# Low parts of W ahead of tile 0's gate, and tile 0's LoRA and tile 1's narrow product inside tile 1's wide product

## Chip, core and metric

The kernel runs on one core of a Trainium2 chip. The metric is the device time of one execution in microseconds (us); the lower the better. Times of the trace are us from the start of the span.

## What is computed

The input x has 1024 rows of 1024 numbers, handled as 8 tiles of 128 rows. First a quantised product with the context is added to x, then an FFN with a top-2 LoRA mixture on the layer-normalised result:

```
x1 = x + fake_quant(layernorm(x)) @ fake_quant(ctx)      # 2 batches, 1024 x 1024 ctx each
y = layernorm(x1)
logits = y @ W_router.T;  combine = renormalised top 2 of softmax(logits)   # 8 experts
h = (y @ A_stack.T) * combine                            # 8 experts x rank 16 = 128 columns
out = x1 + y @ W_base.T + b_base + (h @ B_stack) * 2
```

## The kernel before

There is no scheduler: each engine runs a list of calls written out by hand, in order, and waits on semaphores. An instruction that waits holds up all that stands behind it in its engine's list.

Stage 1 (`product`, L795) makes x1 tile by tile; VectorE adds the product to x (`sum_x1`, L541), and a correction row is added by `add_corr`: for tiles 0 to 2 on VectorE (L550), for tiles 3 to 7 on POOL (L250).

Stage 2 works in float16 pairs: each float32 operand is split into a high part (ScalarE) and a low part (VectorE), and TensorE multiplies high by high, high by low, low by high. For each tile t:

- The layer norm of y: `statistics_y` on VectorE (L464 to L466), `scale_y` on POOL (nine small operations, L261 to L289), `make_y` on ScalarE (L383).
- The transposed y: tiles 0 and 1 are transposed by TensorE (`transpose_y`, L804) and split by `split_first_yt` or `split_yt`. From tile 2 on, ScalarE rounds y to its high part (`round_y`, L402), VectorE makes the low part (`rest_y`, L637), and two DMA transposes of SyncE's queue bring `yt_hi` and `yt_lo` (L205, L207).
- `narrow(t)` (L816 to L818, 24 small matmuls) gives the 128 LoRA columns and 8 logits in one PSUM bank.
- `gate_tile(t)` on VectorE (L642 to L655, with one exp on ScalarE, `gate_weight`, L406) turns the logits into `hc`, which TensorE transposes (`transpose_hc`, L810). `split_hct` splits the result (ScalarE L410, VectorE L662).
- `wide(t, k)` for k = 0 to 7 (L835, 6 matmuls each) is the base product with slice k of W. For tile 0 it waits for `w_lo` of slice k, which VectorE makes from `w_hi` (`split_w`, L606 and L370).
- `lora(t)` (L825, 6 matmuls) adds the LoRA part; then VectorE's `sum_out` (L677) adds the product to x1, `add_bias` (L671) has added the bias, and the tile is stored.

`keep_busy` (L845) issues matmuls whose result is not used, between stage 1 and stage 2. From tile 2 on `narrow(t)` waits for both DMA transposes of its tile. In ScalarE's list before, the step of tile t is:

```
for t in range(1, T):
    gate_weight(t)
    if t + 1 < T:
        make_y(t + 1)
        round_y(t + 1)
    split_hct(t)
```

Of the kernel before, what the change touches and what calls it, by code (L numbers as in the profile page):

```python
# [5 lines left out]
P = 128  # L6
# [3 lines left out]
F32 = mybir.dt.float32  # L10
# [19 lines left out]
def xattn_ffn(nc, x, ctx_kv, quant, w_t, bias, ar_t, b_t, out):  # L30
# [20 lines left out]
    with ExitStack() as stack:  # L51
# [83 lines left out]
        YT_BANKS = slice(6, 8)  # L135
        OUT_BANK = [0, 4]
        AR_BANK = 2
        HCT = slice(256, 256 + P)
        LAST_PIECES = ((0, H), (H, H + H // 2), (H + H // 2, D))
        PEAKS = 2 + K  # L140
        FIRST = 2
        FIRST_ADDS = 3

        quant_in = sem("quant_in")
        x0_half = sem("x0_half")
# [96 lines left out]
        @block.gpsimd  # L242
        def _(pool):
            def fill(tile):
                return nc.gpsimd.memset(tile.rearrange("p t d -> p (t d)").bitcast(U32), OFFSET_PAIR)

            def add_corr(t):
                pool.wait_ge(x1_summed, t + 1)
                pool.wait_ge(corr_ready, t // TB + 1)
                nc.gpsimd.tensor_tensor(xs[:, t, :], xs[:, t, :], corr[:, t // TB, :], ALU.add).then_inc(x1_ready, 1)  # L250

            steps = [0]

# [37 lines left out]

            nc.gpsimd.memset(ident[:, :], 0.0).then_inc(ident_ready, 1)
            pool.wait_ge(ident_ready, 1)
            nc.gpsimd.affine_select(out=ident[:, :], in_=ident[:, :], compare_op=ALU.not_equal, fill=1.0,
                                    base=0, pattern=[[-1, P]], channel_multiplier=1).then_inc(ident_ready, 1)
            then(nc.gpsimd.memset(minus_half[:, :], -0.5))
            for first, last in ((0, 4), (4, 8)):
                fill(a2[:, first:last, :]).then_inc(a2_filled, 1)
            nc.gpsimd.iota(expert_i[:, :], pattern=[[1, EX]], base=0, channel_multiplier=0).then_inc(iota_ready, 1)
            fill(a1[:, 4:8, :]).then_inc(a1_rest_filled, 1)  # L300
            fill(a2[:, 12:16, :]).then_inc(a2_filled, 1)
            pool.wait_ge(consts_ready, 1)
            pool.wait_ge(a1_filled, 2)
            pool.wait_ge(a1_rest_filled, 1)
            scale_x(1, 2)
            for t in range(2, 6):
                scale_x(t, t + 1)
                quantise_x(t)
            scale_x(6, 8)
            quantise_x(6)  # L310
            quantise_x(7)
            scale_y(0, 2)
            pool.wait_ge(b_lo_ready, 1)
            add_corr(3)
            scale_y(2, 3)
            add_corr(4)
            scale_y(3, 4)
            for t in range(5, T):
                add_corr(t)
                scale_y(t - 1, t)  # L320
            scale_y(T - 1, T)

        @block.scalar
        def _(act):
# [82 lines left out]

            def split_hct(t):
                act.wait_ge(hc_transposed, t + 1)
                nc.scalar.activation(hct_hi[:, :], ps[:, AR_BANK, HCT], ACT.Copy).then_inc(hct_hi_ready, 1)  # L410

            act.dma_start(prm[:, :], quant.partition_broadcast(P)).then_inc(quant_in, 16)
            act.wait_ge(ones_ready, 1)
# [19 lines left out]
            split_w(1)  # L433
            split_w(2)
            make_y(1)
            split_b()
            for k in range(3, K):
                split_w(k)
            gate_weight(0)
            split_yt(1)  # L440
            split_hct(0)
            sum_row(0)
            sum_row(1)
            for t in range(1, T):
                gate_weight(t)
                if t + 1 < T:
                    make_y(t + 1)
                    round_y(t + 1)
                split_hct(t)
                if t + 1 < T:  # L450
                    sum_row(t + 1)

        @block.vector
        def _(dve):
# [204 lines left out]

            def split_hct(t):  # L660
                dve.wait_ge(hct_hi_ready, t + 1)
                nc.vector.tensor_tensor(hct_lo[:, :], ps[:, AR_BANK, HCT], hct_hi[:, :].bitcast(F32),  # L662
                                        ALU.subtract).then_inc(hct_lo_ready, 1)

            def add_bias(t):
# [58 lines left out]
            sum_x1(4)  # L724
            take_a1t(6)
            scale_ar()
            add_corr(2)
            sum_x1(5)
            peaks_w()
            take_a1t(7)  # L730
            scale_w()
            split_ar()
            sum_x1(6)
            split_w(0)
            split_first_yt()
            split_w(1)
            split_w(2)
            split_w(3)
            sum_x1(7)
            dve.wait_ge(iota_ready, 1)  # L740
            nc.vector.tensor_copy(expert[:, :], expert_i[:, :]).then_inc(expert_ready, 1)
            split_w(4)
            split_w(5)
            dve.wait_ge(expert_ready, 1)
            gate_tile(0)
            split_w(6)
            split_w(7)
            split_hct(0)
            split_b()
            split_yt(1)  # L750
            statistics_y(2)
            add_bias(0)
            for t in range(1, T):
                gate_tile(t)
                sum_out(t - 1)
                split_hct(t)
                add_bias(t)
                if t + 1 < T:
                    rest_y(t + 1)
                if t + 2 < T:  # L760
                    statistics_y(t + 2)
# [11 lines left out]
        def _(pe):  # L773
# [33 lines left out]

            def transpose_hc(t):
                pe.wait_ge(hc_ready, t + 1)
                nc.tensor.transpose(ps[:, AR_BANK, HCT], hc[:, :], ident[:, :]).then_inc(hc_transposed, 1)  # L810

            def narrow(t):
                dst = ps[:, AR_BANK, 0:AR]
# [80 lines left out]
                    if t + 1 < T and k == 4:  # L894
                        transpose_a1(t + 1)

            keep_busy(6, 5)
            pe.wait_ge(x1_summed, T - 1)
            pe.wait_ge(first_half_lo, 1)
            for k in range(K):  # L900
# [2 lines left out]
                pe.wait_ge(w_lo_ready, k + 1)  # L903
                wide(0, k, False)
                if k == 3:
                    pe.wait_ge(x1_summed, T)
                    pe.wait_ge(yt_lo_ready, 1)
                    pe.wait_ge(ar_lo_ready, 2)
                    narrow(0)
                if k == 3:  # L910
                    transpose_y(1)
                if k == 5:
                    transpose_hc(0)
            pe.wait_ge(b_lo_ready, 1)
            lora(0, stop=True)

            for t in range(1, T - 1):
                if t == 1:
                    pe.wait_ge(yt_lo_ready, 2)
                else:  # L920
                    pe.wait_ge(y_hi_turned, 16 * (t - 1))
                    pe.wait_ge(y_lo_turned, 16 * (t - 1))
                narrow(t)
                if t >= 2:
                    pe.wait_ge(out_summed, t - 1)
                for k in range(K):
                    wide(t, k, k == K - 1)
                    if k == 2:
# [44 lines left out]
```

## Time and profile before

| | us |
|---|---|
| median of 3 runs | 171.85 (171.85 to 171.87) |
| the profiled execution's own time | 171.81 |
| its span, first to last instruction | 170.0 |
| TensorE busy | 158.2 (93%) |
| VectorE busy | 118.9 (70%) |
| ScalarE busy | 74.1 (44%) |
| POOL busy | 59.9 (35%) |
| mean granted TensorE clock, as a share of 2.4 GHz | 0.996 |

The profiled execution took 1.8 us beyond its span. Busy shares are means over the whole span; the stages have different limits, so a stage has to be read from its own stretch.

### The profile page before, as it was taken

How to read it: one execution, taken by the hardware profiler on the slowest of the kernel's cores; microseconds unless marked ns; L12 is line 12 of the kernel's file. 1: busy time of each engine (PE TensorE's matmuls, PEld its weight loads, DVE VectorE, ACT ScalarE, POOL GpSimd, SP SyncE). 2: the span in 40 equal slices, each digit the busy share in tenths (PEclk: the TensorE clock that was granted, in tenths of full speed). 3: DMA queues.
4: the chain of work that ended last, by engine and by line, in shares of the span. 5: the costliest groups of instructions: out<-in, count | busy, mean ns of one | idle time of the engine just before them, and what ended most of it. 6: DMA issues, size and time to landing. Idle time of an engine off the chain costs nothing.

```text
span 170.0 us, 2585 instructions
## 1 busy us (share of the span) xinstructions
PE 158.2 (93%) x922; PEld 83.6 (49%) x922; DVE 118.9 (70%) x276; ACT 74.1 (44%) x100; POOL 59.9 (35%) x140
## 2 busy tenths in 40 slices
PE   6977898899989799799999999999999999999992
PEld 3543344345535356364554564564555556456541
DVE  7993939999998999996919908908907826804802
ACT  3096509799996994506217007105305305300000
POOL 8905476887840000187082081082050050000000
PEclk9999999999999999999999999999999999999998
DMA  4999999999930000000352250350360360360311
GB/s 111 387 416 413 406 409 407 406 411 413 407 151 2 0 0 4 0 0 0 75 177 41 46 160 10 72 169 0 62 185 4 62 185 0 62 185 6 123 62 62
DMA packets 19452, 25.89 MB, mean 152 GB/s; under 512 B 13552, under 2 KB 13808, under 8 KB 19440
## 3 DMA queue, kind: packets, MB, share of 16 engines
q1 hardware_dynamic: 19296, 25.73, 43.4%
q8 instruction: 7, 0.11, 0.3%
q14 instruction: 5, 0.04, 0.1%
q10 hardware_dynamic: 144, 0.00, 0.0%
HBM read 18.38 MB, written 4.19 MB: 133 GB/s over the span
## 4 chain that ended last, share of the span: by engine, by line
PE 62%; DVE 19%; issue 6%; POOL 5%; ACT 4%; DMA 2%; DVEq 0%; ACTq 0%; POOLq 0%
PE ps L835 37%; PE ps L795 10%; PE ps L825 5%; DVE w_lo L606 2%; PE ps L786 2%; DVE xs L541 2%; ACT w_hi L370 2%; DMA yt_lo<-a_t 2%; PE ps L816 2%; PE ps L817 2%; PE ps L818 2%; POOL root L262 2%; PE ps L780 1%; DVE bnx L472 1%; DVE bnx L470 1%
## 5 line engine op out<-in xcount | busy, mean ns | idle before, releaser
L835 PE MATMUL ps<-w_hi,yt_hi 128*128 128x512 f16 x128 | 39.5, 380 | 1.7 <-DVE w_lo L606 1.2
L835 PE MATMUL ps<-w_lo,yt_hi 128*128 128x512 f16 x128 | 39.4, 379 | 0.0
L835 PE MATMUL ps<-w_hi,yt_lo 128*128 128x512 f16 x128 | 39.4, 379 | 0.0
L795 PE MATMUL ps<-a,a_t 128*128 128x512 f16 x128 | 31.2, 379 | 2.3 <-DVE a_t L534 1.5
L406 ACT ACTIVATE gate<-gate,ar_undo 128x1 f32<-128x1 f32 x8 | 2.4, 295 | 55.9 <-DVE gate L643 55.9
L331 ACT ACTIVATE a<-stage,prm,inv_s 128x1024 uint8<-128x1024 f32 x16 | 19.4, 1241 | 9.4 <-DMA stage<-in_ctx_kv 9.3
L642 DVE MAX8 top<-ps 128x8 f32<-128x8 f32 x8 | 1.4, 173 | 27.5 <-PE ps L818 27.5
L835 PEld LDWEIGHTS ps<-w_hi,yt_lo 128*128 128x128 f16 x128 | 12.5, 98 | 15.1
L795 PEld LDWEIGHTS ps<-a,a_t 128*128 128x128 f16 x128 | 11.9, 98 | 16.2 <-DVE a_t L534 3.0
L835 PEld LDWEIGHTS ps<-w_lo,yt_hi 128*128 128x128 f16 x128 | 12.5, 98 | 14.7
L250 POOL TENSOR_TENSOR xs<-xs,corr 128x1024 f32<-128x1024 f32 x5 | 11.8, 2363 | 22.2 <-DVE b_lo L612 22.2
L835 PEld LDWEIGHTS ps<-w_hi,yt_hi 128*128 128x128 f16 x128 | 11.6, 98 | 14.9 <-issue 2.8
L261 POOL TENSOR_SCALAR root<-mvy 128x1 f32<-128x1 f32 (+1 forms) x7 | 1.5, 218 | 38.8 <-DVE mvy L466 38.7
L816 PE MATMUL ps<-ar_hi,yt_hi 128*128 128x136 f16 x64 | 11.7, 223 | 0.2 <-DMA yt_lo<-a_t 0.2
L817 PE MATMUL ps<-ar_lo,yt_hi 128*128 128x136 f16 x64 | 11.7, 223 | 0.0
L818 PE MATMUL ps<-ar_hi,yt_lo 128*128 128x136 f16 x64 | 11.7, 223 | 0.0
L383 ACT ACTIVATE y<-xs,y_bias,y_scale 128x1024 f32<-128x1024 f32 x8 | 9.8, 1228 | 1.8 <-POOL y_bias L289 1.8
L671 DVE SCALAR_TENSOR_TENSOR xs<-xs,row_term,bias_sb 128x1024 f32<-128x1024 f32 x8 | 10.3, 1285 | 0.3
L786 PE MATMUL ps<-a,ones 128*128 128x512 f16 x32 | 9.5, 379 | 0.9 <-ACT a L331 0.9
L606 DVE SCALAR_TENSOR_TENSOR w_lo<-stage,scale,w_hi 128x1024 f16<-128x1024 f32 x8 | 10.0, 1279 | 0.2 <-ACT w_hi L370 0.2
L541 DVE SCALAR_TENSOR_TENSOR xs<-ps,con,xs 128x1024 f32<-128x1024 f32 x8 | 10.1, 1268 | 0.0
L262 POOL TENSOR_TENSOR root<-root,minus_half 128x1 f32<-128x1 f32 (+1 forms) x13 | 9.7, 744 | 1.1
(135 smaller groups left out, 262.4 us busy)
## 6 DMA issues: line engine op xcount, KB each, us to landing
stage<-in_ctx_kv SPq DMA_DIRECT2D x16, 512.0 KB, 13.2
stage<-in_w_t SPq DMA_DIRECT2D x8, 512.0 KB, 10.7
xs<-in_x SPq DMA_DIRECT2D x7, 512.0 KB, 13.2
out_dram<-xs SPq DMA_DIRECT2D x7, 512.0 KB, 3.0
ar_raw<-in_ar_t SPq DMA_DIRECT2D x1, 544.0 KB, 16.3
xs<-in_x SPq DMA_DIRECT2D x2, 256.0 KB, 3.8
b_raw<-in_b_t SPq DMA_DIRECT2D x1, 512.0 KB, 11.3
bias_sb<-in_bias SPq DMA_DIRECT2D x1, 512.0 KB, 12.1
```

The lines of the kernel that those rows point to most:

```text
L250: nc.gpsimd.tensor_tensor(xs[:, t, :], xs[:, t, :], corr[:, t // TB, :], ALU.add).then_inc(x1_ready, 1)
L262: then(nc.gpsimd.tensor_tensor(guess, whole, minus_half[:, w], ALU.pow))
L331: nc.scalar.activation(low_bytes(a2[:, n, :]), stage[:, n % RING, :], ACT.Identity, bias=prm[:, 3:4], scale=inv_s[:, 2:3]).then_inc(ctx_re ...
L541: nc.vector.scalar_tensor_tensor(out=xs[:, t, :].rearrange("p (h n) -> p h n", h=NH), in0=ps[:, s1_bank(t):s1_bank(t) + 2, :], scalar=s12, ...
L606: nc.vector.scalar_tensor_tensor(out=w_lo[:, k, :], in0=stage[:, k, :], scalar=scale[:, 2:3], in1=w_hi[:, k, :], op0=ALU.mult, op1=ALU.sub ...
L671: nc.vector.scalar_tensor_tensor(out=xs[:, t, :], in0=xs[:, t, :], scalar=row_term[:, t:t + 1], in1=bias_sb[:, :], op0=ALU.add, op1=ALU.ad ...
L786: last = nc.tensor.matmul(ps[:, COLSUM_BANK + h, :], ones16[:, 0:P], a2[:, b * K + k, h * H:(h + 1) * H], start=k == 0, stop=k == K - 1)
L795: last = nc.tensor.matmul(ps[:, s1_bank(t) + h, :], a1_t[:, t % 4, k, :], a2[:, n, h * H:(h + 1) * H], start=k == 0, stop=k == K - 1)
L816: nc.tensor.matmul(dst, yt_hi[:, p, k, :], ar_hi[:, k, :], start=k == 0, stop=False)
L817: nc.tensor.matmul(dst, yt_hi[:, p, k, :], ar_lo[:, k, :], start=False, stop=False)
L818: last = nc.tensor.matmul(dst, yt_lo[:, p, k, :], ar_hi[:, k, :], start=False, stop=k == K - 1)
L835: ins = nc.tensor.matmul(ps[:, OUT_BANK[p] + h, :], part, rhs[:, k, h * H:(h + 1) * H], start=k == 0 and part is hi and rhs is w_hi, stop= ...
```

## The change

VectorE no longer adds the correction of tile 2; POOL does, once `w_diag_ready` is set, and on POOL `scale_y` now stands ahead of `add_corr` of the next tile. VectorE makes the low parts of the LoRA and router weights (`split_ar`) after `w_lo` of slice 3, makes all `w_lo` and tile 1's `yt_lo` ahead of tile 0's gate, and reads `a1_t` of tile 7 ahead of `peaks_w`. TensorE runs `narrow(0)` after `wide(0, 5)`, and all of `transpose_hc(0)`, `narrow(1)`, `lora(0)` and `transpose_hc(1)` inside tile 1's wide product; `lora(1)` ends it. The transposed `hc` gets a PSUM bank of its own. For tile 1 alone, `split_hct(1)` stands ahead of `make_y(2)` and `round_y(2)` on ScalarE, and ahead of `sum_out(0)` on VectorE. `keep_busy` issues 2 matmuls in the place of 6.

```diff
-        FIRST_ADDS = 3
+        FIRST_ADDS = 2
...
             scale_y(0, 2)
+            pool.wait_ge(w_diag_ready, 1)
+            add_corr(2)
             pool.wait_ge(b_lo_ready, 1)
-            add_corr(3)
-            scale_y(2, 3)
-            add_corr(4)
-            scale_y(3, 4)
-            for t in range(5, T):
+            for t in range(3, T):
+                scale_y(t - 1, t)
                 add_corr(t)
-                scale_y(t - 1, t)
             scale_y(T - 1, T)
...
             make_y(1)
-            split_b()
             for k in range(3, K):
                 split_w(k)
+            split_yt(1)
+            split_b()
             gate_weight(0)
-            split_yt(1)
             split_hct(0)
             sum_row(0)
             sum_row(1)
             for t in range(1, T):
                 gate_weight(t)
+                if t == 1:
+                    split_hct(t)
                 if t + 1 < T:
                     make_y(t + 1)
                     round_y(t + 1)
-                split_hct(t)
+                if t > 1:
+                    split_hct(t)
...
             scale_ar()
-            add_corr(2)
             sum_x1(5)
+            take_a1t(7)
             peaks_w()
-            take_a1t(7)
             scale_w()
-            split_ar()
             sum_x1(6)
             split_w(0)
             split_first_yt()
             split_w(1)
             split_w(2)
             split_w(3)
+            split_ar()
+            split_w(4)
             sum_x1(7)
...
-            split_w(4)
-            split_w(5)
+            for k in range(5, K):
+                split_w(k)
+            split_yt(1)
             dve.wait_ge(expert_ready, 1)
             gate_tile(0)
-            split_w(6)
-            split_w(7)
             split_hct(0)
             split_b()
-            split_yt(1)
             statistics_y(2)
             add_bias(0)
             for t in range(1, T):
                 gate_tile(t)
-                sum_out(t - 1)
-                split_hct(t)
+                if t == 1:
+                    split_hct(t)
+                    sum_out(t - 1)
+                else:
+                    sum_out(t - 1)
+                    split_hct(t)
...
-            keep_busy(6, 5)
+            keep_busy(2, 5)
...
                 wide(0, k, False)
                 if k == 3:
+                    transpose_y(1)
+                if k == 5:
                     pe.wait_ge(x1_summed, T)
-                    pe.wait_ge(yt_lo_ready, 1)
                     pe.wait_ge(ar_lo_ready, 2)
                     narrow(0)
+
+            pe.wait_ge(yt_lo_ready, 2)
+            for k in range(K):
+                wide(1, k, False)
+                if k == 1:
+                    transpose_hc(0)
+                if k == 2:
+                    narrow(1)
                 if k == 3:
-                    transpose_y(1)
-                if k == 5:
-                    transpose_hc(0)
-            pe.wait_ge(b_lo_ready, 1)
-            lora(0, stop=True)
-
-            for t in range(1, T - 1):
...
+                    pe.wait_ge(b_lo_ready, 1)
+                    lora(0, stop=True)
+                if k == 6:
+                    transpose_hc(1)
+            lora(1, stop=True)
```

On ScalarE, the end of the list for tiles 0 and 1 before: the exp of a gate is L406, the high part of the transposed `hc` L410, `y` of the next tile L383 and its rounding (named `a_t` by the memory it shares) L402.

```order
L406 ACTIVATE gate<-gate,ar_undo 128x1
L394 ACTIVATE yt_hi<-ps 128x1024
L410 ACTIVATE hct_hi<-ps 128x128
L345 ACTIVATE junk,rowsum<-a1 128x1024 x2
L406 ACTIVATE gate<-gate,ar_undo 128x1
L383 ACTIVATE y<-xs,y_bias,y_scale 128x1024
L402 ACTIVATE a1_t<-y 128x1024
L410 ACTIVATE hct_hi<-ps 128x128
L345 ACTIVATE junk,rowsum<-a1 128x1024
```

The same place in the changed kernel, whose lines stand one lower (L405, L409, L382, L401):

```order
L393 ACTIVATE yt_hi<-ps 128x1024
L374 ACTIVATE b_hi<-b_raw 128x1024
L405 ACTIVATE gate<-gate,ar_undo 128x1
L409 ACTIVATE hct_hi<-ps 128x128
L344 ACTIVATE junk,rowsum<-a1 128x1024 x2
L405 ACTIVATE gate<-gate,ar_undo 128x1
L409 ACTIVATE hct_hi<-ps 128x128
L382 ACTIVATE y<-xs,y_bias,y_scale 128x1024
L401 ACTIVATE a1_t<-y 128x1024
L344 ACTIVATE junk,rowsum<-a1 128x1024
```

The high part of tile 1's transposed `hc` has moved ahead of tile 2's `y` and its rounding.

On TensorE, tile 1's wide product (L835) around the transpose of its `hc` (L810), before; the list goes on with the rest of `lora(1)` (L825) and two more slices of W:

```order
L835 MATMUL ps<-w_hi,yt_lo 128x512 x2
L810 MATMUL ps<-ident,hc 128x128
L835 MATMUL ps<-w_hi,yt_hi 128x512 x2
L835 MATMUL ps<-w_lo,yt_hi 128x512 x2
L835 MATMUL ps<-w_hi,yt_lo 128x512 x2
L835 MATMUL ps<-w_hi,yt_hi 128x512 x2
L835 MATMUL ps<-w_lo,yt_hi 128x512 x2
L835 MATMUL ps<-w_hi,yt_lo 128x512 x2
L835 MATMUL ps<-w_hi,yt_hi 128x512 x2
L835 MATMUL ps<-w_lo,yt_hi 128x512 x2
L835 MATMUL ps<-w_hi,yt_lo 128x512 x2
L825 MATMUL ps<-b_hi,hct_hi 128x512 x2
```

The end of tile 1 in the changed kernel, where these are L839, L814 and L829, up to tile 2's narrow product:

```order
L839 MATMUL ps<-w_lo,yt_hi 128x512 x2
L839 MATMUL ps<-w_hi,yt_lo 128x512 x2
L839 MATMUL ps<-w_hi,yt_hi 128x512 x2
L839 MATMUL ps<-w_lo,yt_hi 128x512 x2
L839 MATMUL ps<-w_hi,yt_lo 128x512 x2
L814 MATMUL ps<-ident,hc 128x128
L839 MATMUL ps<-w_hi,yt_hi 128x512 x2
L839 MATMUL ps<-w_lo,yt_hi 128x512 x2
L839 MATMUL ps<-w_hi,yt_lo 128x512 x2
L829 MATMUL ps<-b_hi,hct_hi 128x512 x2
L829 MATMUL ps<-b_lo,hct_hi 128x512 x2
L829 MATMUL ps<-b_hi,hct_lo 128x512 x2
```

The transpose of tile 1's `hc` has moved from behind slice 2 to behind slice 6; one slice and `lora(1)` follow it, and then comes `narrow(2)`.

On VectorE, from the weight scale to tile 0's gate, before (`ar_lo` is `split_ar`, L541 `sum_x1`, L619 tile 0's `yt_lo`, L642 the gate's first operation):

```order
L586 SCALAR_TENSOR_TENSOR ar_lo<-ar_raw,scale,ar_hi 128x8x128
L586 SCALAR_TENSOR_TENSOR ar_lo<-ar_raw,scale,ar_hi 128x8x8
L541 SCALAR_TENSOR_TENSOR xs<-ps,con,xs 128x1024
L606 SCALAR_TENSOR_TENSOR w_lo<-stage,scale,w_hi 128x1024
L619 TENSOR_TENSOR yt_lo<-ps,yt_hi 128x512 x2
L606 SCALAR_TENSOR_TENSOR w_lo<-stage,scale,w_hi 128x1024 x3
L541 SCALAR_TENSOR_TENSOR xs<-ps,con,xs 128x1024
L741 CAST expert<-expert_i 128x8
L606 SCALAR_TENSOR_TENSOR w_lo<-stage,scale,w_hi 128x1024 x2
L642 MAX top<-ps 128x8
```

The same in the changed kernel (L588, L543, L608, L621, L630 for tile 1's `yt_lo`, L644 for the gate):

```order
L543 SCALAR_TENSOR_TENSOR xs<-ps,con,xs 128x1024
L608 SCALAR_TENSOR_TENSOR w_lo<-stage,scale,w_hi 128x1024
L621 TENSOR_TENSOR yt_lo<-ps,yt_hi 128x512 x2
L608 SCALAR_TENSOR_TENSOR w_lo<-stage,scale,w_hi 128x1024 x3
L588 SCALAR_TENSOR_TENSOR ar_lo<-ar_raw,scale,ar_hi 128x8x128
L588 SCALAR_TENSOR_TENSOR ar_lo<-ar_raw,scale,ar_hi 128x8x8
L608 SCALAR_TENSOR_TENSOR w_lo<-stage,scale,w_hi 128x1024
L543 SCALAR_TENSOR_TENSOR xs<-ps,con,xs 128x1024
L743 CAST expert<-expert_i 128x8
L608 SCALAR_TENSOR_TENSOR w_lo<-stage,scale,w_hi 128x1024 x3
L630 TENSOR_TENSOR yt_lo<-ps,yt_hi 128x1024
L644 MAX top<-ps 128x8
```

`split_ar` is now behind four `w_lo`, and the gate begins only after the eighth and after tile 1's `yt_lo`.

## Rows read from the trace of the kernel before

**Rows 1.** Busy time by stretch: us, busy (instructions) of each engine, then clock, DMA
```profile
55.60:87.00 31.40, 29.49 (x178) 15.87 (x177) 27.03 (x52) 16.23 (x22) 9.39 (x17) 1.00 0.12 31
86.70:100.00 13.30, 13.28 (x79) 7.25 (x80) 8.76 (x20) 3.80 (x6) 5.05 (x14) 1.00 0.35 97
```

**Rows 2.** The chain that ended last: start us, us, what
```profile
53.15 0.89 PE ps L804 x8
...
65.22 0.18 DVE top L642
...
67.49 0.29 DVE hc L655
...
72.64 0.60 DVE bny L464
...
77.77 0.22 POOL y_bias L289
...
80.31 0.27 ACT hct_hi L410
...
80.81 0.28 DVE row_term L667
...
82.31 1.23 DVE a_t L637
83.56 3.03 DMA yt_lo<-a_t
...
86.72 0.22 PE ps L816
...
88.30 3.88 PE ps L835 x18
...
96.26 1.39 PE ps L825 x6
```

**Rows 3.** Timeline of TensorE: start us, us, operation, idle before and its releaser
```profile
51.20 0.23 PE L878 MATMUL ps<-diag,ones_b 128*128 128x128 bf16 x1 [0.85 <-DVE a_t L534]
...
57.30 0.59 PE L835 MATMUL ps<-w_hi,yt_hi 128*128 128x512 f16 x2 [0.57 <-DVE yt_lo L619]
...
88.14 0.59 PE L835 MATMUL ps<-w_hi,yt_hi 128*128 128x512 f16 x2
```

**Rows 4.** Timeline of VectorE, same columns
```profile
47.70 1.23 DVE L550 TENSOR_TENSOR xs<-xs,corr 128x1024 f32<-128x1024 f32 x1
...
51.46 0.29 DVE L597 TENSOR_REDUCE power<-ps 128x1 f32<-128x128 f32 x1 [0.32 <-PE ps L878]
...
52.73 1.48 DVE L586 SCALAR_TENSOR_TENSOR ar_lo<-ar_raw,scale,ar_hi 128x1024 f16<-128x1024 f32 x2
...
56.52 1.28 DVE L619 TENSOR_TENSOR yt_lo<-ps,yt_hi 128x512 f16<-128x512 f32 x2
57.71 2.48 DVE L606 SCALAR_TENSOR_TENSOR w_lo<-stage,scale,w_hi 128x1024 f16<-128x1024 f32 x2
```

**Rows 5.** Timeline of ScalarE, same columns
```profile
52.79 1.15 ACT L370 ACTIVATE w_hi<-stage,scale 128x1024 f16<-128x1024 f32 x1 [1.25 <-DVE scale L601]
...
58.24 1.05 ACT L375 ACTIVATE b_hi<-b_raw 128x1024 fp32r<-128x1024 f32 x1
```

**Rows 6.** Timeline of POOL, the add of tile 5's correction
```profile
87.86 2.36 POOL L250 TENSOR_TENSOR xs<-xs,corr 128x1024 f32<-128x1024 f32 x1
```

**Rows 7.** Timeline of VectorE during that add
```profile
88.55 0.21 DVE L643 TENSOR_SCALAR gate<-top 128x1 f32<-128x1 f32 x1
...
88.95 1.30 DVE L646 CAST top_f<-top_i 128x8 f32<-128x8 uint32 x1
```

**Rows 8.** Busy time by stretch at the end of the span
```profile
165.75:167.00 1.25, 0.96 (x5) 0.45 (x3) 0.26 (x1) 0.00 (x0) 0.00 (x0) 1.00 0.00 0
168.50:169.00 0.50, 0.00 (x0) 0.00 (x0) 0.00 (x0) 0.00 (x0) 0.00 (x0) 0.68 0.80 270
```

**Rows 9.** The source line of the first 32 matmuls: duration ns min/median/max, first and last start
```profile
L842 PE MATMUL ps<-ones x32: 326/326/527, 1.4 to 8.1; 128*128 128x384 f16 x32
```

More of the change, by code:

```diff
@@ L137, in xattn_ffn @@
         AR_BANK = 2
-        HCT = slice(256, 256 + P)
+        HCT_BANK = 3
+        HCT = slice(0, P)
         LAST_PIECES = ((0, H), (H, H + H // 2), (H + H // 2, D))
@@ L409, in split_hct @@
                 act.wait_ge(hc_transposed, t + 1)
-                nc.scalar.activation(hct_hi[:, :], ps[:, AR_BANK, HCT], ACT.Copy).then_inc(hct_hi_ready, 1)
+                nc.scalar.activation(hct_hi[:, :], ps[:, HCT_BANK, HCT], ACT.Copy).then_inc(hct_hi_ready, 1)
             act.dma_start(prm[:, :], quant.partition_broadcast(P)).then_inc(quant_in, 16)
@@ L661, in split_hct @@
                 dve.wait_ge(hct_hi_ready, t + 1)
-                nc.vector.tensor_tensor(hct_lo[:, :], ps[:, AR_BANK, HCT], hct_hi[:, :].bitcast(F32),
+                nc.vector.tensor_tensor(hct_lo[:, :], ps[:, HCT_BANK, HCT], hct_hi[:, :].bitcast(F32),
                                         ALU.subtract).then_inc(hct_lo_ready, 1)
@@ L809, in transpose_hc @@
                 pe.wait_ge(hc_ready, t + 1)
-                nc.tensor.transpose(ps[:, AR_BANK, HCT], hc[:, :], ident[:, :]).then_inc(hc_transposed, 1)
+                nc.tensor.transpose(ps[:, HCT_BANK, HCT], hc[:, :], ident[:, :]).then_inc(hc_transposed, 1)
             def narrow(t):
@@ L905, in _ @@
                 if k == 3:
+                    transpose_y(1)
+                if k == 5:
                     pe.wait_ge(x1_summed, T)
-                    pe.wait_ge(yt_lo_ready, 1)
                     pe.wait_ge(ar_lo_ready, 2)
                     narrow(0)
-                if k == 3:
-                    transpose_y(1)
-                if k == 5:
-                    transpose_hc(0)
-            pe.wait_ge(b_lo_ready, 1)
-            lora(0, stop=True)
-            for t in range(1, T - 1):
[L918 to L922, printed above, removed]
+            pe.wait_ge(yt_lo_ready, 2)
[5 more added lines that the diff above has]
+                    narrow(1)
+                if k == 3:
+                    pe.wait_ge(b_lo_ready, 1)
[3 more added lines that the diff above has]
+            lora(1, stop=True)
+            for t in range(2, T - 1):
+                pe.wait_ge(y_hi_turned, 16 * (t - 1))
+                pe.wait_ge(y_lo_turned, 16 * (t - 1))
                 narrow(t)
-                if t >= 2:
-                    pe.wait_ge(out_summed, t - 1)
+                pe.wait_ge(out_summed, t - 1)
                 for k in range(K):
```

## The prediction

> **What bounds the kernel now.** I read the busy time by stretch first. From 86.7 us on TensorE is busy for 13.28 us of 13.30 us [rows 1]: one tile of stage 2, and so on to the end; nothing but fewer or slower matmuls changes that part. Ahead of it, from 55.6 to 87.0 us, where tiles 0 and 1 run, it is busy for 29.49 of 31.40 us. So about 2 us can be had there, and some in the wait just before (below). Then the chain that ended last, which says what sets the start of the full part. It is not TensorE. Through 72.64, 77.77, 80.31, 82.31 and 83.56 us it runs over VectorE's statistics of tile 2, POOL's scale, ScalarE, VectorE's low part of y and the DMA transpose of `yt_lo`, and releases `narrow(2)` at 86.72 us [rows 2]. TensorE had only just finished tile 1: two limits meet here. Any gain in tiles 0 and 1 arrives at 86.72 us only if tile 2's y comes sooner too. The chain also shows that before 86.72 us VectorE had waited for ScalarE's part of tile 1's transposed `hc` (80.31 us) ahead of that low part: the two chains, gate and y, are tied.
>
> **The front of stage 2.** The W peak matmul stood at 51.20 us after 0.85 us of idle, for VectorE's `a1_t` of tile 7 [rows 3]. Without `add_corr(2)` (47.70 us, 1.15 us in the queue beside 1.23 long) [rows 4] and with `take_a1t(7)` ahead of `peaks_w`, VectorE is done in time, and TensorE's own products set the start: 51.20 - 0.85 = 50.3 us, 0.9 us sooner. Everything to the weight scale moves with it. `split_ar` leaves the path: it stood at 52.73 us, 1.48 us long, 1.4 us in the queue [rows 4]. Tile 0's `yt_lo` then starts at 56.52 - 0.9 - 1.4 = 54.2 us, and `wide(0, 0)`, which began 0.78 us behind it (57.30 us [rows 3]), at 55.0 us. With 2 `keep_busy` instead of 6 TensorE is free by then: it was free at 57.30 - 0.57 = 56.7 us, less 0.9, less four of 384 columns at 2.4 GHz, 0.16 us each, gives 55.2 us at most. Gain so far 2.2 us.
>
> **Tiles 0 and 1 on TensorE.** Costs of one: `wide` 3.88 / 3 = 1.29 us, `lora` 1.39, eight transposes of y 0.9 [rows 2]; `narrow` 88.14 - 86.72 = 1.42 us [rows 2, 3]; a transpose of `hc` 0.1 us by the same eight. Waits for `w_lo`, each 1.28 us long and 1.2 us in the queue (two took 2.48 us [rows 4]): slice 1 starts at 54.2 + 1.2 and is ready at 56.7, TensorE wants it at 56.3 (wait 0.4). Slice 3 needs its `w_hi`, which takes the place of `split_b`: 58.24 - 0.9 = 57.3 us, 1.15 us long [rows 5], so `w_lo` is ready at 59.8 against 59.4 (0.4). Slice 4 comes behind `split_ar`, ready at 62.4 against 62.0 (0.4). Slice 5 comes behind `sum_x1(7)`, ready at 64.9 against 63.7 (1.2). Slices 6 and 7 are made while `narrow(0)` runs. Sum of waits 2.4 us; moving the gate behind all `w_lo` does not remove them, since `split_ar` and `sum_x1(7)` still stand between.
>
> Up to the transpose of tile 1's `hc` there are 15 `wide` (19.4), two `narrow` (2.8), one `lora` (1.4), y (0.9) and `hc` (0.1): 24.6 us. It starts at 55.0 + 24.6 + 2.4 = 82.1 us. One `wide` and `lora(1)` remain: TensorE is done with tiles 0 and 1 at 82.1 + 0.1 + 1.3 + 1.4 = 84.9 us.
>
> Is `hc` of tile 1 there by then? Tile 0's transpose, behind two slices of tile 1, is at about 72.8 us, so VectorE's `split_hct(0)` starts at about 73.6; `b_lo` (1.2), statistics (1.5) and `add_bias` (1.5) bring the gate to 77.8, and it takes 67.49 + 0.29 - 65.22 = 2.6 us [rows 2]: 80.4 us. Yes. Tile 2's scale: statistics from 74.8 us, and y_bias came 5.35 us behind their start (72.64 to 77.99 [rows 2]), so 80.2 us, 2 us later than before; hidden, because of the next step.
>
> **The step that decides: `split_hct(1)` ahead of `make_y(2)`.** ScalarE keeps its order, so y of tile 2 cannot be made before the transpose at 82.1 us. Add: 0.3 us to ScalarE's reading it (0.26 us for the peak matmul, 51.20 to 51.46 [rows 3, 4]); from there VectorE's `row_term` came 0.5 us later (80.31 to 80.81), and now `sum_out(0)` stands between, another 1.2 us by an operation of that size; 1.5 us to the low part of y, 1.25 us to its DMA, 3.16 us to `narrow(2)` (80.81, 82.31, 83.56, 86.72) [rows 2]. Sum 0.3 + 0.5 + 1.2 + 1.5 + 1.25 + 3.16 = 7.9 us, so `narrow(2)` starts at 90.0 us. The high part is no later: y and its rounding took 80.31 - 77.99 = 2.3 us, ready at 82.1 + 0.5 + 2.4 = 85.0, and VectorE reaches `rest_y` at 85.6. The two DMAs of SyncE's queue are then some 1.9 us apart, and I take the second's 3.16 us as unchanged; if it waited for the whole of the first, which takes about as long, it would be 1.2 us later. SyncE itself is free: its wait for `lora(0)` ends at about 78 us, and tile 0's store stands behind both. Under this chain TensorE has 2.8 us of work and stands idle for 5.1 us.
>
> So `narrow(2)` is 90.0 - 86.72 = 3.3 us later, with all of tiles 2 to 7 behind it at the old pace: each later tile's y chain starts from its own gate, in the old order. POOL's adds have slack there (2.36 us [rows 6] in a tile of 13.3 us). 171.81 (this execution's own time; 0.04 under the median) + 3.3 = 175.1 us at full clock. Lower bound of this term: no wait for `w_lo` at all gives 79.7 + 7.9 = 87.6, still +0.9, 172.7 us.
>
> **The clock.** After its last matmul, at 165.75 + 0.96 = 166.7 us, TensorE's granted clock was down to half inside the stretch 168.5 to 169.0 us (mean 0.68, so at about 168.7) [rows 8]: after some 2 us without work it went from 2.4 to 1.2 GHz. An idle of 5 us in mid-kernel should see the same, once at least. Price from the start of the kernel: 32 matmuls of 384 columns started from 1.4 to 8.1 us [rows 9], 31 steps in 6.7 us where 0.16 us each makes 5.0: 1.7 us lost before the clock was up (the longest took 527 ns, the median 326). I take 1.6 us; bounds 0, since the rise could come early after the gap, and 3.3, an estimate for a low stretch of twice the length. Sum 171.81 + 3.3 + 1.6 = 176.7 us.
>
> The Trainium skill, "TensorE: Matmul & The Clock Gate", HAM oscillation, says that idle gaps between bursts of matmuls throw the array back to the low clock and that the next burst starts cold. By that rule, with which the tail of this trace agrees, the sum is 176.7; without it, 175.1.
>
> **Rivals.**
> *The clock stays up* (0.17): all as above, 175.1 us. For it: the old kernel's waits, 0.85 and 0.57 us [rows 3], left the clock at 1.00; against it, they are short.
> *POOL's add holds VectorE up* (0.06): `add_corr(2)` now runs from about 50.3 to 52.7 us, beside the scale's small operations on VectorE. In the old trace a cast of 128x8 took 1.30 us and ended as such an add ended, 90.2 us; but a TENSOR_SCALAR of 128x1, the form the scale is made of, took its usual 0.21 us during it [rows 6, 7]. If they do wait, the scale, whose first such operation is due at 51.46 + 0.29 - 0.9 = 50.9 us [rows 4], is 52.7 - 50.9 = 1.8 us later and everything with it: 176.9, or 178.5 with the clock. The Trainium skill, "SBUF — State Buffer", Who interferes with whom, lets `tensor_scalar` among others take the port that VectorE shares with POOL, and speaks against this add there; the 0.21 us row speaks for it.
> *The y chain is less late* (0.04): waits for `w_lo` largely gone, 172.7 to 174.5 us.
> *Faster* (0.04): tile 2's y is there when TensorE ends tile 1 at 84.9 us, so the full part starts 1.8 us sooner: 170.0 us. It decides from a transpose of tile 1's `hc` earlier than 86.72 - 7.9 = 78.8 us, and TensorE's work alone puts it at 79.6. Only a far shorter tail, say the DMA at half its 3.16 us, together with no waits, would do it; nothing in the rows shows either.
>
> **How the numbers follow.** The likeliest case, late y and a fallen clock, has 0.69, 175.6 to 178.2 by the bounds of its clock term; I give 176.7. The range takes in the rival at full clock: 175.0 to 178.2, leaving out the less late, the faster, and part of the POOL case. A change of 0.2%, 0.35 us, is about what a measurement here can tell. Slower by more 0.95, within it 0.01, faster 0.04.
>
> **What would show it.** `wide(0, 0)` near 55.0 us; waits for `w_lo` ahead of slices 1, 3, 4, 5; ScalarE idle until the second transposed `hc` near 82 us with POOL's bias ready at 80; `yt_lo`'s DMA issued near 86.9; TensorE idle from 85 to 90 us, released by that DMA; granted clock under 1.00 around 87 to 93. If `narrow(2)` starts before 87 us I am wrong in the step that decides; if the clock stays 1.00, in the last term.

## The result, and the profile after

The changed kernel takes 177.65 us in the median of 4 runs (177.18 to 178.0), the kernel before 171.85 us. The ratio is 1.0336, with a 95% interval of 1.0311 to 1.0361: slower by 5.8 us. The profiled execution, the longest of the four, took 178.0 us over a span of 176.2 us, 6.2 us more span than before.

The page of the changed kernel, its span and the slices of TensorE and of its clock:

```profile
span 176.2 us, 2577 instructions
...
PE   6997889899999979999359999999999999999992
...
PEclk9999999999999999999966999999999999999999
```

There are two dents. In slices 20 and 21 (84 to 93 us) TensorE is busy for three and five tenths, and in slices 21 and 22 its clock is at six tenths. The waits of TensorE name the first:

```profile
PE ps L820 <- DMA yt_lo<-a_t: 5.0, 1, 5.0
PE ps L839 <- DVE w_lo L608: 1.8, 4, 0.9
```

One wait of 5.0 us, for tile 2's `yt_lo`, and four for `w_lo`. The timeline of TensorE, with the waits in brackets:

```profile
50.33 0.22 PE L882 MATMUL ps<-diag,ones_b 128*128 128x128 bf16 x1
...
55.09 0.59 PE L839 MATMUL ps<-w_hi,yt_hi 128*128 128x512 f16 x2
...
56.83 0.60 PE L839 MATMUL ps<-w_hi,yt_hi 128*128 128x512 f16 x2 [0.29 <-DVE w_lo L608]
...
64.93 0.60 PE L839 MATMUL ps<-w_hi,yt_hi 128*128 128x512 f16 x2 [0.92 <-DVE w_lo L608]
...
82.23 0.27 PE L814 MATMUL ps<-ident,hc 128*128 128x128 f32 x1
...
90.16 0.27 PE L820 MATMUL ps<-ar_hi,yt_hi 128*128 128x136 f16 x1 [4.98 <-DMA yt_lo<-a_t]
```

The peak matmul comes 0.87 us sooner than in [rows 3], stage 2 starts at 55.09 in the place of 57.30 us, and tile 1 is done at 85.18 us (84.56 + 0.62 for its last two matmuls). In the kernel before, it was done at 86.53 us, the start of `narrow(2)` less the idle ahead of it:

```profile
86.72 0.22 PE L816 MATMUL ps<-ar_hi,yt_hi 128*128 128x136 f16 x1 [0.19 <-DMA yt_lo<-a_t]
```

So TensorE is done with tiles 0 and 1 1.35 us sooner. But `narrow(2)` starts at 90.16 in the place of 86.72 us. VectorE ahead of it in the changed kernel, each row with its start and duration as above:

```profile
82.84 0.29 DVE L664 TENSOR_TENSOR hct_lo<-ps,hct_hi 128x128 fp32r<-128x128 f32 x1 [2.58 <-ACT hct_hi L409]
83.05 1.27 DVE L679 SCALAR_TENSOR_TENSOR xs<-ps,con,xs 128x1024 f32<-128x1024 f32 x1
84.24 0.26 DVE L669 TENSOR_SCALAR row_term<-rowsum,con 128x1 f32<-128x1 f32 x1
84.54 1.28 DVE L673 SCALAR_TENSOR_TENSOR xs<-xs,row_term,bias_sb 128x1024 f32<-128x1024 f32 x1
85.74 1.22 DVE L639 TENSOR_TENSOR a_t<-y,a_t 128x1024 f16<-128x1024 f32 x1
```

VectorE sat idle for 2.58 us ahead of `hct_lo` of tile 1, and between that and the low part of tile 2's y (the last row) stand three more operations. ScalarE over the same time:

```profile
82.53 0.28 ACT L409 ACTIVATE hct_hi<-ps 128x128 fp32r<-128x128 f32 x1 [4.10 <-PE ps L814]
82.71 1.23 ACT L382 ACTIVATE y<-xs,y_bias,y_scale 128x1024 f32<-128x1024 f32 x1
84.03 1.06 ACT L401 ACTIVATE a_t<-y 128x1024 f16<-128x1024 f32 x1
```

ScalarE, too, waited for the transpose, and had y rounded at 85.09 us, 0.65 us before VectorE reached the low part. Both lists hold y behind the transpose of `hc`; VectorE's holds it a little longer. Then the clock, by stretches of 1 us (the third number from the end is the granted clock, ahead of the DMA's share and its GB/s):

```profile
88.00:89.00 1.00, 0.00 (x0) 0.00 (x0) 0.36 (x2) 0.00 (x0) 0.43 (x2) 1.00 0.87 169
89.00:90.00 1.00, 0.00 (x0) 0.00 (x0) 0.00 (x0) 0.00 (x0) 0.76 (x4) 0.53 1.13 339
...
94.00:95.00 1.00, 1.00 (x4) 0.32 (x3) 0.89 (x5) 0.96 (x1) 0.00 (x0) 0.50 0.00 0
95.00:96.00 1.00, 1.00 (x4) 0.40 (x3) 0.93 (x4) 0.93 (x1) 0.00 (x0) 0.55 0.03 8
96.00:97.00 1.00, 1.00 (x7) 0.45 (x5) 0.83 (x1) 0.13 (x1) 0.00 (x0) 1.00 0.00 0
```

The clock went from 2.4 to 1.2 GHz at about 89.1 us (a mean of 0.53 over the stretch from 89 to 90 us), 3.9 us after TensorE's last work, and came back at 95.9 us. TensorE worked at 1.2 GHz from 90.16 to 95.9 us, 5.7 us, and did what takes half as long, 2.9 us, at 2.4 GHz. So 3.44 us of late start and 2.9 us of half speed are 6.3 us, against 6.2 us in the span.

### The profile page after: what moved, and what is told of

Read it like the earlier page. It is cut to its first block, busy times and chain, and to the rows that moved or that the text cites. A ratio compares the mean times of both kernels' runs of the same rounds, so it can differ in the third digit from the quotient of the medians.

```text
span 176.2 us, 2577 instructions
## 1 busy us (share of the span) xinstructions
PE 161.3 (92%) x918; PEld 85.4 (48%) x918; DVE 116.8 (66%) x275; ACT 74.1 (42%) x100; POOL 61.1 (35%) x141
## 4 chain that ended last, share of the span: by engine, by line
PE 71%; DVE 16%; POOL 3%; issue 3%; ACT 3%; DMA 2%; DVEq 0%; ACTq 0%; POOLq 0%
PE ps L839 44%; PE ps L799 10%; PE ps L829 6%; PE ps L820 2%; PE ps L821 2%; PE ps L822 2%; PE ps L790 2%; DVE xs L543 2%; DVE w_lo L608 2%; ACT w_hi L369 2%; DMA yt_lo<-a_t 2%; PE ps L784 1%; DVE bnx L474 1%; DVE bnx L472 1%; DVE a L694 1%
## 5 line engine op out<-in xcount | busy, mean ns | idle before, releaser
L839 PE MATMUL ps<-w_hi,yt_hi 128*128 128x512 f16 x128 | 40.2, 386 | 1.8 <-DVE w_lo L608 1.8
L839 PE MATMUL ps<-w_hi,yt_lo 128*128 128x512 f16 x128 | 39.8, 383 | 0.0
L839 PE MATMUL ps<-w_lo,yt_hi 128*128 128x512 f16 x128 | 39.8, 383 | 0.0
L405 ACT ACTIVATE gate<-gate,ar_undo 128x1 f32<-128x1 f32 x8 | 2.4, 295 | 56.5 <-DVE gate L645 56.5
L644 DVE MAX8 top<-ps 128x8 f32<-128x8 f32 x8 | 1.4, 172 | 29.2 <-PE ps L822 29.2
L839 PEld LDWEIGHTS ps<-w_hi,yt_lo 128*128 128x128 f16 x128 | 12.6, 99 | 15.4 <-issue 0.6
L839 PEld LDWEIGHTS ps<-w_lo,yt_hi 128*128 128x128 f16 x128 | 12.7, 99 | 15.2 <-issue 0.8
L839 PEld LDWEIGHTS ps<-w_hi,yt_hi 128*128 128x128 f16 x128 | 11.6, 99 | 15.5 <-issue 3.2
L820 PE MATMUL ps<-ar_hi,yt_hi 128*128 128x136 f16 x64 | 12.8, 234 | 5.0 <-DMA yt_lo<-a_t 5.0
L251 POOL TENSOR_TENSOR xs<-xs,corr 128x1024 f32<-128x1024 f32 x6 | 14.1, 2350 | 1.8 <-DVE diag L556 1.8
L821 PE MATMUL ps<-ar_lo,yt_hi 128*128 128x136 f16 x64 | 12.8, 235 | 0.0
L822 PE MATMUL ps<-ar_hi,yt_lo 128*128 128x136 f16 x64 | 12.8, 234 | 0.0
L608 DVE SCALAR_TENSOR_TENSOR w_lo<-stage,scale,w_hi 128x1024 f16<-128x1024 f32 x8 | 10.0, 1280 | 0.6 <-ACT w_hi L369 0.6
L543 DVE SCALAR_TENSOR_TENSOR xs<-ps,con,xs 128x1024 f32<-128x1024 f32 x8 | 10.1, 1269 | 0.1
L382 ACT ACTIVATE y<-xs,y_bias,y_scale 128x1024 f32<-128x1024 f32 x8 | 9.8, 1227 | 0.0
L820 PEld LDWEIGHTS ps<-ar_hi,yt_hi 128*128 128x128 f16 x64 | 6.6, 103 | 6.2 <-issue 5.4
```

The costliest lines, as they stand in the source:

```text
L382: nc.scalar.activation(y[:, :], xs[:, t, :], ACT.Identity, bias=y_bias[:, t:t + 1], scale=y_scale[:, t:t + 1]).then_inc(y_ready, 1)
L543: nc.vector.scalar_tensor_tensor(out=xs[:, t, :].rearrange("p (h n) -> p h n", h=NH), in0=ps[:, s1_bank(t):s1_bank(t) + 2, :], scalar=s12, ...
L608: nc.vector.scalar_tensor_tensor(out=w_lo[:, k, :], in0=stage[:, k, :], scalar=scale[:, 2:3], in1=w_hi[:, k, :], op0=ALU.mult, op1=ALU.sub ...
L820: nc.tensor.matmul(dst, yt_hi[:, p, k, :], ar_hi[:, k, :], start=k == 0, stop=False)
L821: nc.tensor.matmul(dst, yt_hi[:, p, k, :], ar_lo[:, k, :], start=False, stop=False)
L822: last = nc.tensor.matmul(dst, yt_lo[:, p, k, :], ar_hi[:, k, :], start=False, stop=k == K - 1)
```

## The experiments

All ratios are against the kernel before, run on the same chip in the same session.

**1. ScalarE's order for tile 1 undone alone.**

```diff
                 gate_weight(t)
-                if t == 1:
-                    split_hct(t)
                 if t + 1 < T:
                     make_y(t + 1)
                     round_y(t + 1)
-                if t > 1:
-                    split_hct(t)
+                split_hct(t)
```

> The changed kernel with ScalarE's order for tile 1 undone alone: y of tile 2 and its rounding again stand ahead of the high part of tile 1's transposed hc. Theory A (VectorE's list is the tie: hct_lo(1), sum_out(0), bias, low part of y): y is made from 80.2 us instead of 82.7, but hct_lo(1) still waits for the transpose at 82.2 us and for ScalarE behind the rounding (about 82.6 us), so the low part of y stays at about 85.8 us, narrow(2) at 90.2 us, and the time at 177.6 us. Theory B, my prediction's wording (ScalarE's order is what decides): y is 2.4 us sooner and narrow(2) comes at about 87.8 us, time 174.4 to 175.5 us.

Measured: 177.28 us (176.65 to 178.08), ratio 1.032 (1.0283 to 1.0358). ScalarE's timeline, then VectorE's:

```profile
80.31 1.24 ACT L382 ACTIVATE y<-xs,y_bias,y_scale 128x1024 f32<-128x1024 f32 x1 [1.83 <-POOL y_bias L290]
81.64 1.06 ACT L401 ACTIVATE a_t<-y 128x1024 f16<-128x1024 f32 x1
82.60 0.26 ACT L409 ACTIVATE hct_hi<-ps 128x128 fp32r<-128x128 f32 x1
```

```profile
82.89 0.29 DVE L661 TENSOR_TENSOR hct_lo<-ps,hct_hi 128x128 fp32r<-128x128 f32 x1 [2.58 <-ACT hct_hi L409]
...
85.80 1.22 DVE L636 TENSOR_TENSOR a_t<-y,a_t 128x1024 f16<-128x1024 f32 x1
```

y is made 2.4 us sooner, and the low part is where it was. Theory B falls: ScalarE's order, to which my prediction gave the decision, costs nothing as long as the low part of y stands behind `hct_lo(1)` in VectorE's list. The converse was not run: with VectorE's order alone changed, the low part would wait for ScalarE's rounding, done at 85.09 us in the changed kernel, so by these rows only some 0.7 us could come of it. To free y, both lists have to be changed (experiment 4).

**2. The gap filled with matmuls.**

```diff
             lora(1, stop=True)
+            keep_busy(30, 6)
```

> The changed kernel with 30 matmuls of 384 columns, whose result is not used, between the end of tile 1 and narrow(2): 30 x 0.163 = 4.9 us of work in 5.1 us of idle. Theory A (the loss is 3.4 us of late y plus 2.9 us of half clock after the idle): the clock stays at 1.00, narrow(2) still at 90.2 us, time 171.85 + 3.4 = 175.3 us, about 2.4 us under the changed kernel. Theory B (the clock is not what costs; tile 2 is slower for another reason, such as its operands or the DMA): time stays at 177.6 us.

Measured: 175.8 us (175.66 to 176.07), ratio 1.0235 (1.0218 to 1.0252), 1.9 us under the changed kernel. The start of `narrow(2)` there:

```profile
90.76 0.22 PE L820 MATMUL ps<-ar_hi,yt_hi 128*128 128x136 f16 x1 [0.65 <-DMA yt_lo<-a_t]
```

The granted clock is 1.00 in each stretch from 84 to 97 us, and the part behind is at its old pace: 174.0 - 90.76 = 83.2 us, before 170.0 - 86.72 = 83.3, in the changed kernel 176.2 - 90.16 = 86.0. The cost of the clock is shown: 2.8 us, against 2.9 worked out above. The time fell by 1.9 us only, and misses theory A's 175.3 us by 0.5, since `narrow(2)` is 0.6 us later than in the changed kernel: SyncE's issue of the first DMA transpose took 2.24 us instead of 1.31, and held the second. Why it did, no run settles; another issue took 2.00 us at 148.7 us of the same trace, far from the filling matmuls.

**3. Both orders undone.** Experiment 1, and on VectorE:

```diff
-                if t == 1:
-                    split_hct(t)
-                    sum_out(t - 1)
-                else:
-                    sum_out(t - 1)
-                    split_hct(t)
+                sum_out(t - 1)
+                split_hct(t)
```

> The changed kernel with both orders for tile 1 undone: on ScalarE y(2) and rounding first, on VectorE sum_out(0) ahead of hct_lo(1). Theory A (the late transpose of tile 1's hc is the root, at 82.2 us, and hct_lo(1) holds the low part of y whatever stands ahead of it): sum_out(0) moves into VectorE's idle, worth 1.2 us; low part at 84.5, narrow(2) at 89.0 us, TensorE idle 3.9 us, clock falls still in most runs: 176.2 to 176.6 us. Theory B (the two orders for tile 1 are the cause): undoing them brings the time back to 172 us or less.

Measured: 175.66 us (175.54 to 176.67), ratio 1.0243 (1.0211 to 1.0275). `sum_out(0)` now runs in VectorE's idle, the rest is as late as the transposed `hc`:

```profile
80.18 1.27 DVE L676 SCALAR_TENSOR_TENSOR xs<-ps,con,xs 128x1024 f32<-128x1024 f32 x1
82.85 0.29 DVE L661 TENSOR_TENSOR hct_lo<-ps,hct_hi 128x128 fp32r<-128x128 f32 x1 [1.39 <-ACT hct_hi L409]
```

`narrow(2)` came at 88.96 us as expected, TensorE idle for 3.8 us. The time is 0.5 us under what I expected, since the low clock cost less: it lasted from about 89.7 to 93.0 us. The two orders of the change are worth 1.2 us of `narrow(2)`. The rest is the later transpose, as long as the low part of y stands behind it; experiments 4 and 5 take these two apart.

**4. The low part of y ahead of the gate's chain.** ScalarE as in experiment 1, and on VectorE for tile 1 `rest_y(2)`, `split_hct(1)`, `sum_out(0)`, `add_bias(1)`:

```diff
                 if t == 1:
+                    rest_y(t + 1)
                     split_hct(t)
                     sum_out(t - 1)
...
-                if t + 1 < T:
+                if 1 < t < T - 1:
                     rest_y(t + 1)
```

> The changed kernel with y(2) and rounding first on ScalarE, and on VectorE the low part of y(2) ahead of hct_lo(1), sum_out(0) and the bias; the transpose of hc stays where it is. Theory A (tying the y chain to the gate chain costs the time): the low part runs at 82.7 to 83.9 us, right behind the rounding, its DMA is issued at 83.9, narrow(2) at 87.1 us, idle 1.8 us, clock stays up: 171.85 + 0.4 = 172.2 us (173.5 if the clock still falls). Theory B (the y chain is late by itself, from the statistics on): not below 175 us.

Measured: 172.39 us (172.34 to 172.67), ratio 1.0035 (1.0021 to 1.0049). With ScalarE's order undone and one operation of VectorE moved ahead of four others, 5.3 us of the 5.8 are gone, and the transpose stands where it stood (82.24 us):

```profile
82.78 1.23 DVE L636 TENSOR_TENSOR a_t<-y,a_t 128x1024 f16<-128x1024 f32 x1 [2.51 <-ACT a_t L401]
...
84.25 0.74 PE L827 MATMUL ps<-b_hi,hct_hi 128*128 128x512 f32 x2 [0.45 <-DVE hct_lo L661]
87.38 0.22 PE L818 MATMUL ps<-ar_hi,yt_hi 128*128 128x136 f16 x1 [1.48 <-DMA yt_lo<-a_t]
```

The low part is made at 82.78 in the place of 85.74 us. `lora(1)` waits 0.45 us for the low part of `hc` that now comes second, the idle ahead of `narrow(2)` is 1.48 us, and the clock stays at 1.00.

**5. The transpose of tile 1's hc one slice sooner.**

```diff
-                if k == 6:
+                if k == 5:
                     transpose_hc(1)
```

> The changed kernel with the transpose of tile 1's hc one slice of W sooner, behind slice 5 instead of 6; nothing else. Theory A (the y chain starts at that transpose): it runs at 80.9 instead of 82.2 us, and all behind it 1.3 us sooner: narrow(2) at 88.9 us, idle 3.8 us; 176.3 us if the clock falls as before, 174.0 if it stays up. Theory B (another wait of the chain, POOL's scale ready at 80.2 us, takes over at once): under 0.5 us of gain.

Four executions took 174.02, 175.49, 175.62 and 176.71 us; the ratio, 1.017 (1.012 to 1.0219), is that of the first three. In the profiled one `narrow(2)` starts at 88.91 us after 3.70 us of idle, 1.25 us sooner, as theory A says. The spread is the clock's: the mean granted clocks of the four are 1.0, 0.99, 0.99 and 0.98, and 174.0 is the forecast for a clock that stays up. With an idle of this length the clock's cost differs from execution to execution of one kernel. In the profiled one it fell at about 89.8 us, 0.8 us after TensorE had begun to work again, and was back at about 93.1 us.

**6. y of tile 2 sooner still.** Experiment 4, `transpose_hc(1)` behind slice 4, and `b_lo` and tile 2's statistics in VectorE's idle:

```diff
             gate_tile(0)
-            split_hct(0)
             split_b()
             statistics_y(2)
+            split_hct(0)
             add_bias(0)
```

> The orders of the run with the low part of y(2) first, and besides: b_lo and tile 2's statistics ahead of hct_lo(0) on VectorE, into its 2.6 us of idle there, and the transpose of tile 1's hc behind slice 4. Theory A: statistics end at 73.5 us, POOL's bias at 77.4, rounding at 79.8, low part at 81.0, its DMA lands at 84.2 us, before TensorE ends tile 1 at 85.0 us: no idle there, the full part starts at 85.0 us instead of 86.7, time 170.1 us, faster than both kernels. Theory B (a gain in front of tile 2 is lost again in tile 3, whose statistics now come later against its narrow product): a wait of 0.5 us or more ahead of narrow(3), time 170.7 us or more.

Measured: 172.24 us (172.04 to 172.72), ratio 1.0025 (1.0015 to 1.0035). Neither theory named the cause. The wait for `yt_lo` is gone, but TensorE waits twice for `hc`; beside it, VectorE's gate of tile 1 and POOL:

```profile
80.69 0.33 PE L812 MATMUL ps<-ident,hc 128*128 128x128 f32 x1 [0.89 <-DVE hc L654]
92.39 0.33 PE L812 MATMUL ps<-ident,hc 128*128 128x128 f32 x1 [0.79 <-DVE hc L654]
```

```profile
77.31 2.36 DVE L649 TENSOR_SCALAR c<-expert,top_f,gate 128x8 f32<-128x8 f32 x1
```

```profile
77.26 2.37 POOL L251 TENSOR_TENSOR xs<-xs,corr 128x1024 f32<-128x1024 f32 x1
```

A gate operation that takes 0.29 us alone took 2.36, and ended with POOL's add of tile 3's correction (79.67 and 79.63 us). It is the pattern of [rows 6, 7], now where TensorE waits behind it.

**7. The front of the change alone, in the kernel before.** Add 2 on POOL, `scale_y` ahead of `add_corr`, `take_a1t(7)` ahead of `peaks_w`, 2 filling matmuls:

```diff
             scale_ar()
-            add_corr(2)
             sum_x1(5)
+            take_a1t(7)
             peaks_w()
-            take_a1t(7)
```

> The kernel before with one part of the change alone: add 2 on POOL behind the W peaks, POOL's scale ahead of its add, a1_t of tile 7 ahead of the peaks, 2 filling matmuls. Gates and products as before. Theory A (this removes the 0.85 us wait at the peak matmul and shifts all behind it): 171.85 - 0.9 = 170.95 us. Theory B (the add on POOL beside VectorE's scale, or POOL's new order, gives it back): 171.7 us or more.

Measured: 171.3 us (171.28 to 171.33), ratio 0.9969 (0.9957 to 0.9982). Faster, by 0.55 in the place of 0.9 us. VectorE's scale runs at its pace beside POOL's add (in the changed kernel too, where its last operation took 0.14 us at 51.68 us and the add ran from 50.27 us); `split_ar`, which still stands behind it here, does not:

```profile
50.30 2.36 POOL L250 TENSOR_TENSOR xs<-xs,corr 128x1024 f32<-128x1024 f32 x1 [1.81 <-DVE diag L552]
```

```profile
51.70 0.14 DVE L599 TENSOR_SCALAR scale<-scale 128x1 f32<-128x1 f32 x1
51.88 2.05 DVE L584 SCALAR_TENSOR_TENSOR ar_lo<-ar_raw,scale,ar_hi 128x1024 f16<-128x1024 f32 x2
```

`split_ar` took 2.05 us, before 1.48 [rows 4]. It overlapped the add, which ended at 52.66 us, by 0.78 us and took 0.57 us longer. So tile 0's `yt_lo` starts 0.28 us sooner (56.24 in the place of 56.52) and not 0.85; TensorE's waits for `w_lo`, 1.0 us in the place of 1.2, give some of it back.

**8. The adds of POOL wait for the gates.** Experiment 6, and on POOL:

```diff
                 scale_y(t - 1, t)
+                pool.wait_ge(*((y_lo_ready, 1) if t == 3 else (hc_ready, t - 1)))
                 add_corr(t)
```

> The orders of the run with y sooner, whose first gate operation on 128x8 took 2.36 and 2.31 us beside POOL's adds of tiles 3 and 4, with one thing more: POOL's add of tile 3 waits until the low part of y(2) is made, and the adds of tiles 4 to 7 until the gate two tiles before is through. Theory A (the port that VectorE and POOL share is all that held that run at 172.2 us): both waits of TensorE for hc (0.9 and 0.8 us) go, tile 1 ends at 85.0 us, the full part starts there and keeps its pace: 170.1 to 170.3 us. Theory B (the shifted statistics and adds of tiles 3 on cost as much elsewhere): 171.5 us or more.

Measured: 170.07 us (170.06 to 170.1), ratio 0.9894 (0.988 to 0.9908). The gate's operation is back at 0.29 us, TensorE's waits for `hc` are gone, and the expected time is met to 0.1 us. That these waits came from VectorE and POOL holding each other up is shown. It goes the other way round too: beside VectorE's `add_bias(0)` (74.82 to 76.11 us), a POOL operation that takes 0.19 us elsewhere took 1.03:

```profile
75.13 1.03 POOL L266 TENSOR_SCALAR root<-root 128x1 f32<-128x1 f32 x1
```

The moved add of tile 3 now stretches `add_bias(1)` to 1.91 us from 1.28, where TensorE does not wait behind it.

**9. All low parts of W in one row.** Experiment 8, and:

```diff
-            split_w(3)
+            for k in range(3, K):
+                split_w(k)
             split_ar()
-            split_w(4)
             sum_x1(7)
...
             split_yt(1)
+            statistics_y(2)
             dve.wait_ge(expert_ready, 1)
             gate_tile(0)
             split_b()
-            statistics_y(2)
             split_hct(0)
```

`narrow(0)` moves behind slice 7, `transpose_hc(0)` behind slice 2 and `transpose_hc(1)` behind slice 5 of tile 1, and POOL's `scale_y(2, 3)` no longer waits for `b_lo`.

> As the run with waiting adds, and the 2.4 us of waits for w_lo attacked: VectorE makes w_lo of all 8 slices ahead of split_ar and sum_x1(7), narrow(0) stands behind slice 7, tile 2's statistics ahead of tile 0's gate, POOL's scale no longer waits for b_lo, the transpose of hc(0) and narrow(1) behind slice 2 of tile 1, that of hc(1) behind slice 5. Theory A (the waits for w_lo come from the two operations between the slices): waits of 0.4 us at slices 1 and 3 alone, tile 1 ends at 83.5 us, yt_lo lands at 83.5 us, narrow(2) at 83.5 us, tile 3's y up to 0.3 us late: 171.85 - 86.7 + 83.6 + 0.3 = 169.0 us. Theory B (one of the chains of y or of the gates, now 1.5 us shorter of cover, takes over): 170.0 us or more.

Measured: 168.59 us (168.54 to 168.84), ratio 0.9811 (0.9796 to 0.9826): 3.2 us under the kernel before. TensorE's waits for `w_lo` in experiment 9:

```profile
PE ps L835 <- DVE w_lo L605: 0.6, 2, 0.3
```

Two waits are left of four, those ahead of slices 1 and 3. `narrow(2)` starts at 83.50 us, right behind tile 1, and from there TensorE has no wait. Theory A again, 0.4 us better than expected, since tile 3's y was not late.

## Why the prediction was right

The time of 177.65 us lies in the range, and the likeliest case is the one that happened: late y and a fallen clock. It is 0.95 us above the forecast of 176.7, and that is mostly the clock term, which was sized too small. Step by step:

- **The front.** Expected `wide(0, 0)` at 55.0, measured 55.09 us. The scale on VectorE was not held up by POOL's add: its TENSOR_SCALAR of 128x1 took 0.14 us beside it, in the changed kernel and in experiment 7, so that rival is out for the operations it named. Two other forms were held up: the TENSOR_SCALAR of 128x8 in the gate, 2.36 for 0.29 us (experiment 6), and `split_ar`, which reads two inputs from SBUF, 2.05 for 1.48 us (experiment 7). The Trainium skill ("SBUF — State Buffer", Who interferes with whom) says that a `tensor_scalar` can contend with POOL when its operands meet certain conditions, which the prediction left out, and that an instruction with two SBUF inputs contends with a POOL instruction that reads SBUF. The 2.36 and 2.05 us agree with that.
- **Waits for `w_lo`.** Ahead of slices 1, 3, 4 and 5 as worked out, the largest at slice 5. The timeline shows 1.8 us of idle; by the starts of the slices they come to 2.5 us, against 2.4 expected (a matmul's modelled end lies behind the next one's start). Experiment 9 took away the two operations between the slices and with them the last two waits.
- **Transpose of tile 1's hc, end of tile 1.** Expected 82.1 and 84.9, measured 82.23 and 85.18 us. (The sum 55.0 + 24.6 + 2.4 is 82.0; the 0.1 moves nothing.)
- **The step that decides.** The size was right: 7.9 us from the transpose to `narrow(2)`, measured 7.93, hence 3.4 us late. The reason as I put it, "ScalarE keeps its order, so y of tile 2 cannot be made before the transpose", is true but names only one of two ties, and the one that ends 0.65 us before the other. Experiment 1 undoes it and gains nothing beyond the spread; experiment 4, with VectorE's order changed too, gains 5.3 us. My sum ran over VectorE's rows already; the heading and the sentence above it did not.
- **The clock.** It fell, as taken; the size was off. I took 1.6 us from the start of the kernel; here it was 2.9 by the trace and 2.8 by experiment 2. TensorE worked for 5.7 us at the low clock, against some 3.4 us there, twice the 1.7 us lost. That one is inferred from the pace of the matmuls alone, since the granted clock of those stretches reads 1.00. The cost varies: in the profiles of experiments 3 and 5 the low clock lasted about 3.4 us. The moment of the fall was off as well: the tail of [rows 8] had it 2 us after the last work, here it was 3.9 us. The bounds of this term do not give the range stated: 175.1 + 0 and 175.1 + 3.3 are 175.1 and 178.4, not 175.6 and 178.2. The measured time lies within either. The Trainium skill, "TensorE: Matmul & The Clock Gate", HAM oscillation, has the burst behind an idle gap start at the low clock; here the trace agrees (0.50 from 90 us on), while in experiments 3 and 5 the first 0.7 us or so of work still had the full one.
- **Tiles 2 to 7.** At the old pace: behind the clock's return nothing is lost, and experiment 2 gives 83.2 us from `narrow(2)` to the end, before 83.3.

What the change meant to do it did: TensorE was through tiles 0 and 1 by 85.18 us, 1.35 us sooner. It put the transpose of tile 1's `hc` so far back, for `narrow(1)` and `lora(0)` to fit in, that the next tile's y, tied behind it in the lists of VectorE and ScalarE, came 5 us too late for TensorE. Untied, and with POOL's adds out of the gates' way, the same ideas are worth 3.2 us.

## What to carry to other kernels

When work moves later in one engine's list, look at what stands behind its reader in the next engine's list, and whether that is on the way to the next tile; here one subtraction of 0.29 us, with three operations behind it, held the low part of y. Look at every engine that feeds the tile: undoing ScalarE's order alone gained nothing. In these runs an idle of TensorE of 3.7 to 5 us mostly cost more than itself, because the clock fell; one of 1.5 us cost only itself. Where operations of VectorE and POOL were seen to stretch each other, place the long one where the other has nothing urgent: a wait on POOL gained 2.2 us (experiment 8 against 6).

## What the runs showed that I had not expected

- The low clock lasted from 89.1 to 95.9 us in the changed kernel, but only from about 89.7 to 93.0 us in experiment 3, with 3.8 us of idle. There, and in experiment 5, the clock fell when TensorE was already at work again, 0.7 to 0.8 us after `narrow(2)` had begun. The kernel of experiment 5, whose idle is 3.7 us, took 174.02 to 175.62 us in three executions and 176.71 in a fourth; experiments 8 and 9, without a gap, spread by 0.04 and 0.3 us.
- A TENSOR_SCALAR of 128x8 on VectorE took as long as a whole POOL add beside it (2.36 us), one of 128x1 did not (0.21 us in [rows 7]).
- Issuing tile 2's first DMA transpose took SyncE 2.24 us in experiment 2, and 1.31 in each other run. Its cause stays open.
